# A graph-network layer on one core: the one-hot destination picks move from two ScalarE activations to one VectorE comparison of 16-bit integers, and the softmax pass runs its maxima ahead of its scatter

## The reference

```
def mesh_conv(x, src, dst, ea, w1, b1, g, bt, w2, b2):
    m = concatenate([x[dst], x[src], ea], -1) @ w1 + b1
    m = silu(group_norm(m, g, bt))
    m = m @ w2 + b2
    out = segment_sum(m, dst); cnt = segment_sum(ones, dst)
    return out / clip(cnt, 1)[:, None]
h = mesh_conv(...); h = silu(group_norm(h)); h = h + time vector
h = mesh_conv(...); h = silu(group_norm(h)); h = h + x
q, k, v = h @ qw + qb, h @ kw + kb, h @ vw + vb        # 8 heads of 16
logits = (q[dst] * k[src]).sum(-1) * scale + (ea @ ew + eb)
amax = segment_max(logits, dst); pe = exp(logits - amax[dst])
w = pe / segment_sum(pe, dst)[dst]
o = segment_sum(w * v[src], dst) @ ow + ob
return x + h + group_norm(o)
```

## Time and profile before

| | |
|---|---|
| time before, median of 3 runs | 8551.26 us (8549.6 to 8553.6) |
| time of the profiled execution | 8545.18 us |
| its span, first to last instruction | 8543.4 us |
| busy: TensorE / VectorE / ScalarE / GpSimd | 6370.7 / 5559.4 / 4605.3 / 4629.7 us |
| granted TensorE clock over the span | 0.753 |
| conv pass 1 and 2 | about 225 to 2240 us, and 2505 to 4560 us |
| logits pass, softmax pass | about 4783 to 6957 us, and 7010 to 8417 us |

### The profile page before, as it was taken

How to read it: one execution, slowest core, us unless ns; L and a number is a source line. 1 busy time by engine, 2 the same in 40 slices (tenths; PEclk the granted TensorE clock), 3 DMA queues, 4 the chain that set the end, 5 groups by cost and what they waited for, 6 DMA issues and landing times. The chain is left out here.

```text
span 8543.4 us, 249109 instructions
## 1 busy us (share of the span) xinstructions
PE 6370.7 (75%) x43500; PEld 4258.2 (50%) x43501; DVE 5559.4 (65%) x14407; ACT 4605.3 (54%) x7842; POOL 4629.7 (54%) x4730
## 2 busy tenths in 40 slices
PE   1788888888648888888884677777666658888884
PEld 1455555555435555555553434343333337776664
DVE  5667676777656666677776566666666666665556
ACT  3445555555334555555552567777777765555542
POOL 0777777777427777777772477777666520000000
PEclk9999999999869999999996655555555555555555
DMA  4445445555225445445451577777666545444442
GB/s 151 134 135 134 135 134 133 134 135 134 73 62 135 134 133 135 135 134 133 134 134 45 162 214 217 215 215 204 194 184 178 167 121 167 156 148 143 135 133 74
DMA packets 1002205, 1233.71 MB, mean 144 GB/s; under 512 B 305427, under 2 KB 647422, under 8 KB 1000674
## 3 DMA queue, kind: packets, MB, share of 16 engines
q1 hardware_dynamic: 776358, 718.99, 28.5%
q0 software_dynamic: 225792, 514.10, 22.5%
HBM read 1091.01 MB, written 141.49 MB: 144 GB/s over the span
## 5 line engine op out<-in xcount | busy, mean ns | idle before, releaser
L823 POOL DMA_INDIRECT conv_rows<-src_table,conv_idx x3136 | 3105.4, 990 | 955.2 <-issue 919.4
L1243 POOL DMA_INDIRECT lg_rows<-kv_table,lg_idx x1568 | 1482.8, 946 | 792.8 <-issue 594.2
L663 PE MATMUL ps<-dst_parts,lg_pick 128*128 x5268 | 668.3, 304 | 671.9 <-ACT lg_pick L648 668.0
L743 PEld LDWEIGHTS ps<-conv_vals,conv_hot 128*128 128x128 f32 x7024 | 916.0, 191 | 504.9 <-issue 349.7
L743 PE MATMUL ps<-sm_vals,sm_hot 128*128 128x136 f32 x3512 | 952.2, 452 | 202.9 <-DVE acc L729 137.7
L887 ACT ACTIVATE conv_sq<-ps 128x512 f32<-128x512 f32 x784 | 468.1, 597 | 1108.2 <-PE ps L853 1010.0
L663 PEld LDWEIGHTS ps<-dst_parts,lg_pick 128*128 x5268 | 522.1, 132 | 1052.3 <-issue 1021.1
L847 PE MATMUL ps<-conv_rows,ident_b 128*128 128x512 bf16 x2352 | 646.8, 384 | 523.6 <-DMA conv_rows<-src_table,conv_idx 478.3
L926 DVE TENSOR_REDUCE conv_var<-conv_sq 128x32 f32<-128x512 f32 x784 | 536.5, 684 | 760.3 <-ACT conv_sq L887 734.6
L743 PE MATMUL ps<-conv_vals,conv_hot 128*128 128x129 f32 x7024 | 938.6, 276 | 108.8 <-DVE acc L729 104.2
L1391 DVE CUSTOM_DVE_ANT_0 acc<-ps,acc 128x512 f32<-128x512 f32 x976 | 635.4, 689 | 549.9 <-ACT acc L1306 497.5
(11 more groups left out here) (223 smaller groups left out, 9447.7 us busy)
## 6 DMA issues: line engine op xcount, KB each, us to landing
conv_dst<-dst_rows SPq DMA_DIRECT2D x784, 256.0 KB
acc<-dst_rows SPq DMA_DIRECT2D x392, 256.0 KB
v_edges<-lg_rows SPq DMA_DIRECT2D x392, 256.0 KB
sm_dst<-dst_rows SPq DMA_DIRECT2D x392, 256.0 KB, 3.3
sm_v<-v_edges SPq DMA_DIRECT2D x392, 256.0 KB, 2.6
conv_rows<-src_table,conv_idx POOLq DMA_INDIRECT x3136
conv_ea<-ea_parts SPq DMA_DIRECT2D x784, 36.0 KB
lg_rows<-kv_table,lg_idx POOLq DMA_INDIRECT x1568
```

Of the source, the lines that this page charges most:

```text
L663: last = pe.matmul(to[:, j, :], names, part, start=False, stop=False, skip_group_check=True)
L743: last = pe.matmul(bank(SUMS[g])[:, 0:self.width], self.hot[g][:, j, :], vals[:, j, 0:self.width], start=(j == 0), stop=(j == TILES - 1))
L823: pool.indirect_dma_start(rows[r][:, j, :], None, src_table, bass.IndirectOffsetOnAxis(idx[r][:, j:j + 1], 0)).then_inc(S["rows_in"][r], 16)
L1243: pool.indirect_dma_start(rows[r][:, j, :], None, kv_table, bass.IndirectOffsetOnAxis(idx[r][:, j:j + 1], 0)).then_inc(S["rows_in"][r], 16)
```

## The change

1. `pick_dve` replaces `pick_act` in all four passes: one VectorE `tensor_scalar` with `is_equal`, from the destination row to the one-hot in bf16. The row is now a 16-bit integer in DRAM and SBUF, 128 KB instead of 256 KB per broadcast.
2. The pick stands at the end of VectorE's slot body, with a load of the range word of its own. At the start of the next slot `picked_all` waits until all picks are made and reports to SP, which reloads the destination buffer.
3. In the logits pass SP waits for that report too, and the destination rows get buffers of their own.
4. In the softmax pass TensorE does the picked maxima before the scatter products.

```diff
-        dst_rows = dram("dst_rows", [SUPERS, SUPER])
+        dst_rows = dram("dst_rows", [SUPERS, SUPER], I16)
...
-                hold(act, picks.made, q, S["act_paced"])
-                act.activation(apart, dst, ACT.Square, bias=neg_node[:, bass.ds(blk, 1)]).then_inc(picks.apart_made, 1)
-
-                act.wait_ge(picks.used, q)
-                hold(act, picks.apart_made, q, S["act_paced"])
-                act.activation(picks.buffer(act, turn), apart, ACT.Relu, bias=one_col[:, 0:1], scale=-1.0).then_inc(picks.made, 1)
...
+                dve.wait_ge(*ready)
+                hold(dve, picks.used, q, S["dve_paced"])
+                dve.tensor_scalar(picks.buffer(dve, turn), dst, node_of[:, bass.ds(blk, 1)], None, ALU.is_equal).then_inc(picks.made, 1)
+                next_pair(dve, reg, turn)
+            pairs(dve, ends, body)
+
+        def picked_all(dve, S, picks, counters):
+
+            hold(dve, picks.made, value(dve, counters[0], 1), S["picked"])
...
@@ conv, softmax_pass, and the same in logits_pass: VectorE's body
                         def body(stage):
+                            if stage(1):
+                                picked_all(dve, S, picks, picked)
...
+                            if stage(0):
+                                s, r, k = stage(0)
+                                pick_dve(dve, S, picks, picked, span("dve", s)[0], dst[r][:, :], (S["dst_in"][r], 16 * (k + 1)))
                         slots(dve, SCATTER, body)
...
@@ logits_pass, SP
                                 hold(sp, S["query"], s - (DEPTH - 1), S["sp_paced"])
-                                sp.dma_start(dst[r], dst_rows[bass.ds(s, 1), :].to_broadcast([P, SUPER])).then_inc(S["dst_in"][r], 16)
+                                hold(sp, S["picked"], s - (DEPTH - 1), S["sp_paced"])
+                                sp.dma_start(dst[r][:, :], dst_rows[bass.ds(s, 1), :].to_broadcast([P, SUPER])).then_inc(S["dst_in"][r], 16)
...
@@ softmax_pass, TensorE's body
-                            if stage(SCATTER):
-                                s, r, k = stage(SCATTER)
-                                scatter.products(pe, scattered, far, r, vals[r], (S["vals"], s + 1))
                             if stage(MAXIMUM):
...
                                 pe.matmul(maxima, digit_w[:, :], zeros[:, :], start=False, stop=True,
                                           skip_group_check=True).then_inc(S["maxima"], 1)
+                            if stage(SCATTER):
+                                s, r, k = stage(SCATTER)
+                                scatter.products(pe, scattered, far, r, vals[r], (S["vals"], s + 1))
```

More of the change, by code:

```diff
@@ L620, in __init__ @@
                 self.tag, self.buffers = tag, buffers
-                self.made, self.used, self.apart_made = (sem(f"{tag}_{x}") for x in ("pick", "pick_free", "apart"))
+                self.made, self.used = (sem(f"{tag}_{x}") for x in ("pick", "pick_free"))
             def counters(self, eng):
@@ L876, in _ @@
                     def _(act):
-                        picked = picks.counters(act)
-                        act.sem_inc(picks.made, 1)
                         def body(stage):
-                            ends = stage(0) and span("act", stage(0)[0])[0]
                             if stage(SQUARE):
@@ L900, in _ @@
                     def _(dve):
[L901 removed]
+                        scattered, before, picked = scatter.counters(dve), [counter(dve, f"{tag}_before", 0)], picks.counters(dve)
+                        dve.sem_inc(picks.made, 1)
                         dve.sem_inc(picks.used, 2)
```

74 lines of the change are left out of this document (34 added, 40 removed).

## The result

| | before | after |
|---|---|---|
| median of 4 runs each, same chip | 8550.43 us (8544.97 to 8553.6) | 9365.57 us (9362.48 to 9366.63) |
| ratio, 95% interval | | 1.0953 (1.0934 to 1.0972) |
| span of the profiled execution | 8543.4 us | 9363.8 us |

The account below looks back on a forecast made before the run. Gathers were taken to bound the conv and early logits passes, ScalarE late logits, TensorE softmax. 8545 + 248 + 40 + 35 + 5 + 30 - 45 = 8858 us, with 6 us for the median 8864 us; range 8640 to 9230 us.

Parts of the forecast that it names:

- The pick's length: VectorE's 16-bit comparison of 512 elements in all passes: 0.36 us, with ends of 0.22 and 0.75 us.
- Rival 2: VectorE's comparison runs one element at a time, 0.75 us a pick; total about 9395 us; chance 0.10.
- What goes with the pick: VectorE's range load and loop: an operation behind them starts about 0.9 us after the previous issue, plus 0.05 us.
- Softmax term: Softmax pass: VectorE's slot grows to 3.8 us and passes TensorE's 2.97 us; with second blocks +248 us.
- TensorE's 2.97 us bound: Softmax pass before the change: TensorE's scatter products and maxima take 2.97 us a slot and set the pass.
- Conv terms: Conv passes: VectorE's 4.7 us slots on average covered by the gathers' 5.13 us; 20 us a pass, +40 us.
- gathers waiting for TensorE: Sign of a wrong forecast: such waits from a conv pass's start would mean VectorE's 4.7 us is too low.
- Gathers against the pick: VectorE's picks and GpSimd's gathers delay each other: +35 us conv, +5 us early logits, +30 us for shifted moments.
- Rival 3: Each pick stops a gather for its length: 281 us more conv, 55 logits; about 9200 us; chance 0.12.
- Logits term: Logits pass: ScalarE relieved of 1.4 us a pick, late VectorE slots 4.8 us; 1312 against 1357 us, -45 us.
- Maxima first: Softmax pass, TensorE's new order: removes VectorE's 0.40 us wait on the maxima, buys nothing more.
- The range: Total time 8640 to 9230 us: holds the forecast and rival 3, leaves out rivals 1, 2 and 4.

Follow-up runs that it names:

- experiment 2: Changed kernel with the pick comparing 128 of a group's 512 destinations, other three quarters left at zero: 9355.56 us.
- experiment 5: Softmax order swapped: changed kernel with scatter products first, 1.0477 of before (longer-gather chip), softmax 1947 us; kernel before with maxima first, 8576.71 us, 1.0036.

## Why the prediction was wrong

- **The pick's length: right.** 0.36 us forecast, 0.353 median. Rival 2 (0.75 us) falls. But experiment 2 shows that this number decided nothing.
- **What goes with the pick: the step that failed.** The forecast put product to pick at 0.90 us and pick to next comparison at 0.36 + 0.05 + 0.85 = 1.26 us. The rows of one slot show 1.04 and 1.60 us, and comparison to reduction 1.10 for 1.05: 4.29 in place of 3.74 us; a turn of the loop, once in four slots, adds 0.44 us (2.04 against 1.60). The price of a load and a loop, 0.85 to 0.90 us, was nearly right: from the start of the load to the comparison the median is 0.90 us now and 0.87 us in the kernel before. What was put at almost nothing is the pick's own steps behind it (buffer, counter, end of its loop, report), which the earlier trace rows did not have: the forecast let the next load start 0.41 us after the pick, and it starts 0.70 us after it (8306.79 to 8307.49 in the slot above), though the pick is over at 0.35 us. That is 0.29 of the 0.55 us; 0.14 us more lie between product and pick, the rest in the small steps.
- **Softmax term** +248, measured +482. From 7400 to 9200 us, 287 slots with one comparison and one pick take 4.30 us on average, from reduction to reduction; 392 x 4.3 = 1686 us. A second comparison adds 3.36 us and a second pick 1.03 us (forecast 3.5 for both): 47 x 4.39 = 206 us. Sum 1892 us against 1878 measured. The cause, TensorE's 2.97 us bound passed to VectorE, was as forecast.
- **Conv terms** +40 for the slots; with the gathers +105 forecast for both passes, +265 measured. The same mis-sized step (between the last root and the reduction of the next slot the list has nine new rows, not the eight I counted):

```profile
1503.55 0.23 DVE L213 SCALAR_TENSOR_TENSOR conv_rstd<-conv_root_p,conv_rstd 128x64 f32<-128x64 f32 x1
1504.60 0.45 DVE L641 TENSOR_SCALAR conv_pick<-conv_dst,node_of 128x512 int16 x1 [0.83 <-issue]
1505.56 0.35 DVE L641 TENSOR_SCALAR conv_pick<-conv_dst,node_of 128x512 int16 x1 [0.51 <-issue]
1506.18 0.69 DVE L918 TENSOR_REDUCE conv_var<-conv_sq 128x32 f32<-128x512 f32 x1 [0.27 <-DVE conv_pick L641]
...
1508.72 0.29 DVE L726 TENSOR_TENSOR acc<-ps,acc 128x129 f32 x1
1509.53 0.35 DVE L641 TENSOR_SCALAR conv_pick<-conv_dst,node_of 128x512 int16 x1 [0.53 <-issue]
1510.15 0.69 DVE L918 TENSOR_REDUCE conv_var<-conv_sq 128x32 f32<-128x512 f32 x1 [0.26 <-DVE conv_pick L641]
```

From the last root (1503.55) to the first pick 1.05 us, from pick to the next slot 0.62 us, from an addition to the pick 0.81 us. A slot without roots is 3.94 us (3.49 forecast), one with roots 6.30 us (5.71 forecast), means of 144 and 142 slots of pass 1 with one comparison and one pick. Their mean is 5.12 us, which is the 5.13 us of the gathers to 0.01. So there was no cover left, and each second comparison (2.5 us) and second pick (0.96 us) is paid in full: 47 x 3.5 = 163 us at most, 132 measured. The forecast named "gathers waiting for TensorE" as the sign of a 4.7 us that is too low, and the 265 us of the group above are it, from about 800 us on.
- **Gathers against the pick** +35, +5 and +30: nothing. The mean went from 990 to 986 ns. Rival 3 falls. By the Trainium skill, "SBUF — State Buffer", section "Who interferes with whom", a two-port `tensor_scalar` locks GpSimd out for its whole length; a few picks are longer than 353 ns (0.45 us in the rows above, at most 0.60), so the two may hold each other up there, but no run here separates it, and it does not reach the gathers' mean.
- **Logits term** -45: +62. Same step: 4.8 us forecast for one couple and one pick, 5.08 us early and 5.09 us late (counted from product to product). A second couple adds 2.1 us (2.0 forecast), a second pick 1.0 us (0.5 forecast). With the pick behind the dots reduction the slot is 4.80 us and the pass wins 41 us: the sign was a matter of 0.3 us a slot, which the place of the pick decides.
- **Maxima first, counted as the 0.40 us wait gone:** right that it buys nothing in the kernel before, where alone it costs 27 us. In the changed kernel the new order is worth 69 us (experiment 5).
- **The range.** Its upper end came from the price of the pick and of the gathers, both of which turned out harmless, and not from the price of the instruction work, which I had read from one row and given no bounds.

## What to carry to other kernels

Before moving a small operation to an engine that looks idle, count what it brings in loads, registers, branches and semaphore steps, before it and behind it, and price each part from the distance of two starts in rows that have the same steps; busy time hides it. An engine that is busy half its slot can be full. Give that price a range of its own, compare slot and bound as a sum (here 5.12 against 5.13 us), and try the operation in two places: the place was worth 99 us in the logits pass, nothing in the softmax pass, and cost about 60 us in each conv pass.

## What the runs showed of the hardware

On four of the six chips of the experiments the kernel before took 11,442 to 11,544 us (medians), on two 8544 and 8548 us. The softmax pass was the same within 1.2 us for the same kernel; the passes with gathers were 900 us longer. The DMA queues of the changed kernel on both kinds of chip (share of 16 engines over the span):

```profile
q1 hardware_dynamic: 776358, 513.07, 20.4%
q0 software_dynamic: 225792, 514.10, 20.2%
```

```profile
q1 hardware_dynamic: 776358, 513.07, 15.6%
q0 software_dynamic: 225792, 514.10, 15.2%
```

20.4% of 9363.8 us and the share there of 12027.7 us are the same busy time within 4%: the packets take no longer. But between 500 and 1500 us engines of the changed kernel wait there for transfers (the tensor named as releaser can be an earlier owner of the semaphore); the last of these waits is 1.5 us on the other kind of chip, the first is not in its list:

```profile
ACT conv_sq L880 <- DMA w_edge<-w_parts_d: 572.6, 60, 11.5
POOL conv_rows L820 <- issue: 252.9, 454, 5.2
POOL conv_rows L820 <- DMA conv_idx<-in_src_idx: 168.0, 42, 5.6
```

So the passes with gathers wait more for transfers on these chips, in single waits of up to 11.5 us. Which transfers are late the traces do not show: they have no landings of the gathers, and the landings that they do have are the same on both (values 2.6 us, destination rows 2.9 us, medians in the softmax pass). Why these chips differ stays open.
